# Pass 0 of a recurrent attention and ternary feed-forward kernel, rescheduled on eight cores of Trainium2

## What is computed

```
xn = (x - mean) / sqrt(var + 1e-5)
q, k, v = xn @ Wq + bq, xn @ Wk + bk, xn @ Wv + bv
qf, kf = elu(q) + 1, elu(k) + 1
out = (qf @ state + causal(qf kf^T) v) / (qf . sum of kf + 1e-6)
s = out @ Wo + bo
scale = mean(|W|);  T = clip(round(W / scale), -1, 1)
g = silu((layernorm(xn) * ln_w + ln_b) @ T)
y = x + s * g
```

## Time and profile before

| | us |
|---|---|
| runs | 2546.78, 2550.54, 2825.92 |
| median of the runs | 2550.54 |
| profiled execution | 2535.86 |
| its span, slowest core | 2534.3 |
| spans of the eight cores | 2526.8 to 2534.3 |
| TensorE busy in the span | 2410.5 (95%) |

### The profile page before, as it was taken

One profiled execution on the slowest core, in us unless ns is written; L12 is line 12 of the kernel. 1 busy time (PEld: TensorE's weight loads), 2 busy tenths in 40 slices (PEclk: granted clock), 3 DMA queues, 4 the chain that ended last, 5 costly groups with the idle time before them and its releaser, 6 DMA issues.

```text
span 2534.3 us, 39052 instructions; the slowest of 8 cores (2526.8 to 2534.3 us)
## 1 busy us (share of the span) xinstructions
PE 2410.5 (95%) x12749; PEld 1168.0 (46%) x13002; DVE 1370.7 (54%) x2414; ACT 813.6 (32%) x1458; POOL 254.3 (10%) x452
## 2 busy tenths in 40 slices
PE   1798989899999999999999999999999999999998
PEld 0344444444444455554444455554444445554443
DVE  2414887765542367765553167766454247766443
ACT  0134556531210255551110055553110035554000
POOL 1000000011210000001111000001111000000110
PEclk9899999999999999999999999999999999999999
DMA  9896555458885533238896543326888553322651
GB/s 192 204 249 145 122 153 175 117 148 209 210 197 92 103 60 64 68 94 203 209 205 127 94 94 59 77 52 156 235 187 185 96 94 67 68 63 64 169 159 71
DMA packets 158500, 338.20 MB, mean 133 GB/s; under 512 B 78432, under 2 KB 78432, under 8 KB 150112
## 3 DMA queue, kind: packets, MB, share of 16 engines
q0 software_dynamic: 56320, 201.36, 38.7%
q1 hardware_dynamic: 101120, 134.24, 18.8%
q10 hardware_dynamic: 864, 0.10, 0.0%
HBM read 411.14 MB, written 41.94 MB: 179 GB/s over the span
## 4 chain that ended last, share of the span: by engine, by line
PE 87%; DMA 5%; DVE 2%; issue 2%; ACT 2%; SPq 1%; DVEq 0%; ACTq 0%; POOL 0%; POOLq 0%
PE pj L836 48%; PE pj L850 32%; DMA stg<-w_f 4%; SPq L265 1%; DMA xln<-x 1%; PE po L900 1%; PE px L864 1%; PE po L903 1%; PE px L890 1%; PE pa L871 1%; PE px L880 1%; PE pj L930 1%; ACT stg L498 1%; DVE bst L574 0%; DVE tern L706 0%
## 5 line engine op out<-in xcount | busy, mean ns | idle before, releaser
L836 PE MATMUL pj<-ring,big 128*128 128x512 bf16 x6017 | 1331.2, 381 | 76.1 <-DMA big<-xn 68.6
L836 PEld LDWEIGHTS pj<-ring,big 128*128 128x128 bf16 x6144 | 601.8, 98 | 796.4 <-issue 83.6
L850 PE MATMUL pj<-big,ring 128*128 128x512 bf16 x3970 | 905.1, 380 | 17.8 <-ACT er L460 10.8
L850 PEld LDWEIGHTS pj<-big,ring 128*128 128x128 bf16 x4096 | 391.8, 98 | 447.0 <-issue 22.4
L458 ACT ACTIVATE ee<-pj,bq 128x512 f32<-128x512 f32 x128 | 87.8, 686 | 540.7 <-PE pj L850 538.9
L594 DVE TENSOR_TENSOR big<-pj,brow 128x512 bf16<-128x512 f32 x128 | 87.8, 689 | 314.1 <-PE pj L836 294.7
L721 DVE SCALAR_TENSOR_TENSOR tf<-pj,r,c_b 128x512 f32<-128x512 f32 x128 | 95.4, 749 | 236.3 <-PE pj L836 225.5
L554 ACT ACTIVATE sg<-tf 128x512 bf16<-128x512 f32 x128 | 79.7, 629 | 328.3 <-DVE tf L721 328.1
L393 POOL DMA_DIRECT2D ring<-w_qk x128 | 69.0, 557 | 946.7 <-PE pj L850 639.3
L635 DVE TENSOR_TENSOR_SCAN cum<-kh,kc 128x512 f32<-128x512 bf16 x128 | 163.2, 1275 | 0.0
L458 ACT ACTIVATE ee<-pj,bk 128x512 f32<-128x512 f32 x128 | 87.8, 686 | 207.3 <-PE pj L850 207.3
(11 more groups left out here) (67 smaller groups left out, 1591.0 us busy)
## 6 DMA issues: line engine op xcount, KB each, us to landing
ring<-w_qk POOLq DMA_DIRECT2D x128, 512.0 KB, 11.3
xln<-x SPq DMA_DIRECT2D x32, 1024.0 KB, 7.5
ring<-w_v POOLq DMA_DIRECT2D x64, 512.0 KB, 14.7
stg<-w_f SPq DMA_DIRECT2D x32, 1024.0 KB, 7.3
ring<-wscf POOLq DMA_DIRECT2D x64, 512.0 KB, 8.2
ring<-w_o POOLq DMA_DIRECT2D x64, 512.0 KB, 10.7
xy<-x SPq DMA_DIRECT2D x128, 256.0 KB, 4.5
y<-xy POOLq DMA_DIRECT2D x128, 256.0 KB, 4.9
```

The lines of the kernel that those rows point to most:

```text
L836: last = tensor.matmul(bank[:, :], src(k, m), ring[c % 3][:, k * 512:(k + 1) * 512], start=(k == 0), stop=(k == NT - 1))
L850: last = tensor.matmul(bank[:, :], ring[c % 3][:, base + k * 256:base + k * 256 + 128], x[:, k * T + tok:k * T + tok + 512], start=(k == 0 ...
```

## The change

x tiles of pass 0 load into four buffers (xln and stg) and are transposed by TensorE through four psum tiles (px, pa, po), copied to `xbuf(0)` by ScalarE. Chunk 1 waits for ln_apply(2), chunk 2 for group 5. The identity has a semaphore of its own. The absolute sums stand at groups 17, 19, ..., 29 and slots 1, 3, ..., 17. The threshold moves to slot 20, the ternary pieces to slots 22 + 4.75b, that is 22, 26, 31, 36, 41, 45, 50, 55, 60 in q/k and 64, 69, 74, 79, 83, 88, 93 in f/o. For each piece GpSimd multiplies its four 512-column parts by their ln_b and adds them to an accumulator in c_b (`constants`); three slots after the fourth piece of n an fp32 matmul with ones_f over 128 partitions sums and spreads it. lnb3, its splitting and the 16-matmul groups are gone. The layer norms of pass 1's tiles stand at n = 2 and 3 only, in f and o groups alike. All engines' programs are rewritten as one loop over the groups i. Cut to its core:

```diff
-SCALE_SLOT = 15
+SCALE_SLOT = 20
 def tern_slot(b):
-    return 17 + (11 * b) // 4
-def c_slot(n):
-    return tern_slot(4 * n + 3) + 2
+    return 22 + (19 * b) // 4
 TERN_AT = {tern_slot(b): b for b in range(16)}
-C_AT = {c_slot(n): n for n in range(4)}
-B_AT = {c_slot(n) + 1: n for n in range(4)}
+B_AT = {tern_slot(4 * n + 3) + 3: n for n in range(4)}
+def abs_step(a):
+    return 17 + 2 * a if a < 7 else QK0 + 2 * (a - 7) + 1
+ABS_AT = {abs_step(a): a for a in range(16)}
+def ln_step(p, m):
+    if p == 0:
+        return FO0 + 16 * (2 + m // 4) + 1 + 4 * (m % 4)
+    return FO0 + 16 * (m // 2) + 8 + 4 * (m % 2)
+LN_AT = [{ln_step(p, m): (p + 1) * MT + m for m in range(MT)} if p + 1 < NP else {}
+         for p in range(NP)]
+def of_fo(i):
+    n, m = divmod(i - FO0, 16)
+    return n, m % 8, m >= 8
...
+                xfirst = xln + stg
...
+        ptr = pxt + [t.ap().bitcast(BF16) for t in (pa, po)]
...
+            def load_first(m):
+                if m >= 4:
+                    sync.wait_ge(s_xn, m - 3)
+                sync.dma_start(out=xfirst[m % 4][:, :],
+                               in_=x_in[m * 128:(m + 1) * 128, :]
+                               ).then_inc(s_x[m % 4], 16)
             def load_x(g):
-                if g >= 2:
-                    sync.wait_ge(s_xn, g - 1)
+                if g % MT == 0:
+                    sync.wait_ge(s_nrm, g // MT * 32)
+                sync.wait_ge(s_xn, g - 1)
                 sync.dma_start(out=xln[g % 2][:, :],
                                in_=x_in[g * 128:(g + 1) * 128, :]
                                ).then_inc(s_x[g % 2], 16)
...
+                if g == MT:
+                    sync.wait_ge(s_wst[0], 8 * 16)
+                    sync.wait_ge(s_wst[1], 8 * 16)
+                    sync.wait_ge(s_acc, 16)
+                if m == 0 and p > 1:
+                    sync.wait_ge(s_mm, (p - 1) * NG)
                 sync.wait_ge(s_xn, g + 1)
...
                         sync.wait_ge(s_wst[a % 2], 16 * (a // 2))
+                        sync.wait_ge(s_acc, a - 1)
                 elif a >= 2:
                     sync.wait_ge(s_abs, a - 1)
+                else:
+                    sync.wait_ge(s_xn, MT)
...
+            def ternary(i):
+                t = i - QK0
+                if i in ABS_AT and ABS_AT[i] >= 2:
+                    load_piece(ABS_AT[i], 0)
+                if i == 15:
+                    sync.wait_ge(s_mm, 14)
+                    load_piece(0, 0)
+                    load_piece(1, 0)
+                if t == SCALE_SLOT - 1:
                     load_piece(0, 1)
                     load_piece(1, 1)
...
+                if t - 1 in TERN_AT:
+                    store_piece(TERN_AT[t - 1])
+                if t - 4 in TERN_AT and TERN_AT[t - 4] + 2 < 16:
+                    load_piece(TERN_AT[t - 4] + 2, 1)
+            load_first(0)
+            load_first(1)
+            load_bias(0, 0)
+            load_first(2)
+            load_first(3)
+            load_bias(0, 1)
+            for m in range(4, MT):
+                load_first(m)
+            for p in range(NP):
+                for i in range(NG):
+                    if p == 0:
+                        ternary(i)
+                    if i in (8, 16, 24, 32):
+                        load_bias(p, i // 8 + 1)
+                    if i < FO0:
+                        continue
+                    n, m, o = of_fo(i)
+                    if not o and m < 4:
                         load_xr(p, n, m)
...
+                    if o and 2 <= m < 6:
+                        load_xr(p, n, m + 2)
+                    if i + 5 in LN_AT[p]:
+                        load_x(LN_AT[p][i + 5])
+                    if i - 2 in LN_AT[p]:
+                        transpose_x(LN_AT[p][i - 2])
+                    if o and m == 7:
+                        if n < 2:
+                            load_bias(p, 6 + n)
+                        elif p + 1 < NP:
+                            load_bias(p + 1, n - 2)
...
+            def constants(b):
+                n, q = divmod(b, 4)
+                acc = c_b[:, n * 512:(n + 1) * 512]
+                gpsimd.wait_ge(s_ter, b + 1)
+                part = [stg[b % 2][:, 1024 + 512 * i:1536 + 512 * i] for i in range(2)]
+                for i in range(4):
+                    k = q * 4 + i
+                    piece = tern[q][:, i * 512:(i + 1) * 512]
+                    if k == 0:
+                        chained(gpsimd.tensor_scalar(acc, piece, lnb[:, 0:1], None,
+                                                     ALU.mult))
+                        continue
+                    chained(gpsimd.tensor_scalar(part[i % 2], piece, lnb[:, k:k + 1],
+                                                 None, ALU.mult))
+                    last = gpsimd.tensor_tensor(acc, acc, part[i % 2], ALU.add)
+                    if i < 3:
+                        chained(last)
+                last.then_inc(s_acc, 1)
+                gpsimd.wait_ge(s_acc, b + 1)
+            load_chunk(0)
+            gpsimd.wait_ge(s_xn, 3)
+            load_chunk(1)
+            gpsimd.wait_ge(s_mm, 6)
+            load_chunk(2)
+            gpsimd.wait_ge(s_ini, INI_ALL)
+            for p in range(NP):
+                for i in range(NG):
+                    if p == 0 and i - 1 - QK0 in TERN_AT:
+                        constants(TERN_AT[i - 1 - QK0])
+                    c = p * NCHUNK + (i + 1) // 8 + 2
+                    if i % 8 == 7 and c < NP * NCHUNK:
+                        load_chunk(c)
+                    k = p * NG + i - 1
+                    if k > FO0 and (k % NG == NG - 1 or i - 1 >= FO0):
+                        n, m, o = of_fo(k % NG)
+                        if o:
+                            store_y((k // NG * 4 + n) * 8 + m)
...
+            def copy_x(m):
+                for half in range(2):
+                    scalar.wait_ge(s_tr, 2 * m + half + 1)
+                    last = scalar.copy(
+                        xbuf(0)[:, :].rearrange("p (i t) -> p i t", t=T)[
+                            :, half * 8:half * 8 + 8, m * 128:(m + 1) * 128],
+                        blocks(ptr[(2 * m + half) % 4][:, :]))
+                last.then_inc(s_xc, 1)
+            scalar.dma_start(out=identb[:, :], in_=identb_in[:, :]).then_inc(s_id, 16)
...
+            ln_rs(0)
+            ln_rs(1)
             for m in range(MT):
...
+                copy_x(m)
+                if m + 2 < MT:
+                    ln_rs(m + 2)
             scalar.wait_ge(s_ini, INI_ALL)
...
             for p in range(NP):
...
+                for i in range(NG):
+                    t = i - QK0
+                    if QK0 <= i < FO0:
+                        evict_qk(p, t)
+                    if 0 <= t <= LAST_SLOT:
+                        attention(p, t)
+                    if i >= FO0:
+                        n, m, o = of_fo(i)
+                        if not o:
+                            silu(p, n, m)
                     if p == 0:
...
+                        ternary(i)
+                    if i in LN_AT[p]:
+                        ln_rs(LN_AT[p][i])
...
+                if 2 <= g < MT + 2:
+                    vector.wait_ge(s_tr, 2 * (g - 1))
+                elif g >= MT + 2:
+                    vector.wait_ge(s_xt[i], 16 * ((g - MT) // 2))
+                vector.tensor_scalar(xn[i][:, :], xs[:, :], mv[i][:, 0:1],
...
-                    vector.wait_ge(s_cmm, n)
+                    vector.wait_ge(s_acc, b - 3)
...
             ln_stats(0)
+            ln_stats(1)
             ln_apply(0)
             vector.wait_ge(s_ini, INI_ALL)
...
             for p in range(NP):
...
+                for i in range(NG):
+                    t = i - QK0
+                    if p == 0 and i + 2 < MT:
+                        ln_stats(i + 2)
+                    if p == 0 and i + 1 < MT:
+                        ln_apply(i + 1)
+                    if i < QK0:
+                        evict_v(p, i // 8, i % 8)
+                    if 0 <= t <= LAST_SLOT:
+                        attention(p, t)
+                    if QK0 <= i < FO0:
+                        finish_qk(p, t)
+                    if i >= FO0:
+                        n, m, o = of_fo(i)
+                        if o:
+                            evict_o(p, n, m)
+                        else:
+                            evict_f(p, n, m)
                     if p == 0:
                         if t == SCALE_SLOT - 1:
                             threshold()
                             threshold_out()
                         if t in TERN_AT:
                             ternary(TERN_AT[t])
...
+                    if i in LN_AT[p]:
+                        ln_stats(LN_AT[p][i])
+                    if i - 1 in LN_AT[p]:
+                        ln_apply(LN_AT[p][i - 1])
...
-                if t in C_AT:
-                    n = C_AT[t]
-                    bank = take_bank(("c", n))
```

(52 more changed lines are left out.)

199 lines of the change are left out of this document (33 added, 166 removed).

## The result

The changed kernel takes 2630.97 us (median of 4 runs) where the kernel before takes 2548.66 in runs beside it: 1.032 times as long, with a 95% interval of 1.027 to 1.038. The forecast was no change (2550 us, range 2505 to 2590), so it was wrong, in sign and outside its range.

A forecast was written before the change was run, and what follows sets the result against it. TensorE was taken as busy almost throughout except in pass 0. Start +9.3, q/k -28.0 and f/o +26.2 gave +7.5: execution 2543.4 us, 2558 on the median's scale; forecast 2550, between the two, range 2505 to 2590.

The forecast's parts named there:

- Step 1: Start of pass 0: group 0 starts at 38.4 us instead of 55.7, gain 17.3 us; the small load of lnb is late next.
- Step 2: Groups 0 to 7 of pass 0: TensorE and VectorE take turns, period 12.0 us; group 7 9.3 us later than before.
- Step 3: Absolute sums spread over ScalarE's slots: the 10.8 us wait goes; late w_f loads cost 0, at worst 5 us.
- Step 4: Ternary pieces every 4.75 slots, nine in q/k: waits at L890 of 12.4 us for 20.0 before.
- the phase model: Ternary pieces in q/k: one at an even slot costs 2.07 us of wait at L890, at an odd slot 0.51.
- Step 5: Constant row on GpSimd: 14.2 us of matmuls go; a 10 us chain per piece adds waits, 6.5 in q/k, 21.3 in f/o.
- The third rival: VectorE and GpSimd hold each other up: chain 2.8 us longer (+14), prod slower (+5), execution 2562 us; chance 0.13.
- Step 6: Other moves, such as pass 0's layer norms to n = 2 and 3 and later chunk loads, cost nothing.

The follow-up runs named there:

- the fastest version: Changed kernel with ternary part undone, w_f loads two slots behind, VectorE's eviction one group late, its small-load wait at group 32: 2508.7 us, ratio 0.9838 to the kernel before.
- the late eviction alone: Changed kernel with VectorE evicting group i-1 instead of i in the first eight groups of pass 0: 2584.6 us, ratio 1.0167 to the kernel before.
- The odd-slot run: Changed kernel with the ternary pieces in q/k at odd slots alone: 2626.0 us.
- the run without sums: Changed kernel with GpSimd's multiplications and additions left out, a one-column fill signalling each piece: 2558.3 us, one execution.
- the run with short loads: Changed kernel with six of pass 1's eight x tile loads bringing 256 of 2048 columns: 2594.6 us.

## Why the prediction was wrong

The sum was a span of 2541.8 us, and it is 2630.9: 89.1 more. By steps:

**Step 1, right in its reason.** The wait for the small load came, with lnb landing at 35.5 us for an assumed 32.47. Group 0 started at 41.5, predicted 38.4. With the wait moved behind the loop it came at 36.1 in the fastest version, late eviction and all, where the late eviction alone had it at 46.9.

**Step 2, right.** The turns are there, a period of 11.6 us for 12.0, and group 7 at about 112 for 112.6. PE's timeline:

```profile
52.18 1.81 PE L1011 MATMUL px<-identb_s,xn 128*128 128x128 bf16 x16 [5.12 <-DVE xn L670]
53.79 4.56 PE L907 MATMUL pj<-ring,big 128*128 128x512 bf16 x16
63.41 1.01 PE L1011 MATMUL pa<-identb_s,xn 128*128 128x128 bf16 x8 [5.06 <-DVE xn L670]
```

q/k starts 8.7 us later; 9.3 was predicted. The run with the late eviction shows the reason to be the queue order.

**Step 3, nearly.** The wait for ScalarE went, and 6.0 us for kh came at the start of q/k, where 0 was taken and 5 allowed. It doesn't hang on GpSimd's sums: it is 0.8 to 6.9 us by core with them and up to 5.7 without.

**Step 4, a size.** Twelve waits of 16.3 us for nine of 12.4; 2.1 of it lie behind the end of q/k. The odd-slot run took the waits of 2.07 us away, as the phase model has it, but others came, so the model isn't confirmed.

**Step 5, the mechanism right and its main term mis-sized.** The term is the chain per piece, 10 us. GpSimd's timeline of one of 16 pieces:

```profile
564.50 1.56 POOL L458 TENSOR_SCALAR stg<-tern,lnb_s 128x512 f32<-128x512 bf16 x1 [0.89 <-DVE tern L794]
566.21 1.58 POOL L460 TENSOR_TENSOR c_b<-c_b,stg 128x512 f32<-128x512 f32 x1
567.97 1.81 POOL L458 TENSOR_SCALAR stg<-tern,lnb_s 128x512 f32<-128x512 bf16 x1 [0.17 <-POOL c_b L460]
569.92 1.26 POOL L460 TENSOR_TENSOR c_b<-c_b,stg 128x512 f32<-128x512 f32 x1
...
576.20 1.26 POOL L460 TENSOR_TENSOR c_b<-c_b,stg 128x512 f32<-128x512 f32 x1
```

From 564.50 to 577.46, 13.0 us. The twelve chains of eight instructions took 12.9 to 14.2 us, 13.5 on average. By the rule of the prediction (1 + 1 + 1 + 2 us of wait per us of chain) 3.5 us more give 3.5, 3.5, 3.5 and 7.0 on top of 3.1, 3.4, 5.7 and 15.6. Measured were 5.36, 6.75, 9.27 and 22.74: 44.1 us in place of 27.8, within 1.3 us each. My upper bound of 11.6 was no bound, having been taken from VectorE's slowest pass: GpSimd's multiplication of bf16 by a scalar per partition takes 1.56 us alone, more than its own addition of two fp32 tiles at 1.26. The estimate by the Trainium skill (GPSIMD Engine Reference, Performance versus the Vector engine), 12.2 us, was nearer; its ratio of 1.96 for an addition is 1.83 here (1.26 to 0.69).

The third rival, that VectorE and GpSimd hold each other up, came true beside it, in both directions: kh 970 for 682 ns, and a mean of 1794 ns for GpSimd's multiplication in q/k where 1.56 us is its time alone. The Trainium skill (SBUF - State Buffer, Who interferes with whom) has it as an exclusive lock. The rows agree as to who is held up, down to am, which is spared. I priced it at 19 us, and that was too much. Four multiplications of 1.56, four additions of 1.26 and seven gaps of 0.17 make a chain of 12.5 us alone, so the hold-up added 0.4 to 1.7 us to each chain; for the last chain ahead of each of the four bound matmuls that is an estimate of some 5 us by the same rule, and at most 2 us come at z, by the run without sums. The price was of VectorE's instructions and not of TensorE's waits. q/k came out at 313.8 us where 297.9 were predicted: 5.6 more at the bound, 1.8 at z, 6.0 for kh, and 2.0 because the fp32 matmuls behind the waits took 2.04 us for each n where 1.05 was taken from the earlier trace rows, make 15.4 of the 15.9.

**Step 6, wrong, and the largest part.** "The rest costs nothing" held that layer norms of pass 0 moved to n = 2 and 3 are hidden, since VectorE has time there. I weighed VectorE's time and not that of the DMA engines, which had a share of 0.78 over f/o before. Eight megabyte loads and eight transposes now fall in 32 groups instead of 64, beside loads and stores that were there already. The move is forced: x of pass 1 is written over the buffers of the ternary pieces, and these now last into f/o. It cost core 3 34.7 us there, and the run with short loads shows that these loads are the cause: the wait is gone on seven cores of eight. 16.05 us of the same kind came at the end of pass 2, which core 3 shares with one other core. There SyncE stood ahead of the loads of x until a store of y had landed:

```profile
SPq L349 <- DMA y<-xy: 25.6, 1, 25.6
```

That second wait stands beside no edit of pass 0, and what sets it off there wasn't tried.

f/o took 306.6 us where 250.0 were predicted, 56.6 more. Waits at the bound make 10.7 of them (32.0 for 21.3), the wait for x 34.7, other evictions 2.5, the last z wait 2.1. Nearly all of the 6.6 us left is TensorE's own busy time, 235.1 us where the prediction's terms without waits make 228.7: 2.0 are the slower fp32 matmuls, and the rest is other work at the lower of its two clock levels behind these waits (PEclk 0.88).
